# A score and value stage of one fused kernel: one factor ahead, a gram matrix in 32-column blocks, a softmax in halves

## The reference, cut to what matters

```python
xn = _inorm(xa, norm1_w, norm1_b)
k = _fno_layer(xn, Kcw, Ksw, Hs, Ws)
q = _fno_layer(xn, Qcw, Qsw, Hs, Ws)
v = _fno_layer(xn, Vcw, Vsw, H, W)
scores = jnp.einsum('bntk,bnsk->bnts', qf, kf) / (np.float32(np.sqrt(Hs * Ws)) * temperature)
p_attn = jax.nn.softmax(scores, axis=-1)
av = jnp.einsum('bnts,bnsk->bntk', p_attn, vf)
p = _fno_layer(av, Pcw, Psw, H, W)
```

## Time and profile before

| what | us |
|---|---|
| median of 3 runs | 1069.66 |
| lowest, highest | 1069.3, 1073.97 |
| the profiled execution, its own time | 1070.72 |
| its span, first to last instruction | 1069.1 |
| score stage, first load issue to the meeting | 113.7 to 186.8 |
| value stage | 186.9 to 373.5 |

### The profile page before, as it was taken

How to read it: one execution, slowest core, us unless ns; L and a number is a source line. 1 busy time by engine, 2 the same in 40 slices (tenths; PEclk the granted TensorE clock), 3 DMA queues, 4 the chain that set the end, 5 groups by cost and what they waited for, 6 DMA issues and landing times. The chain is left out here.

```text
span 1069.1 us, 36892 instructions
## 1 busy us (share of the span) xinstructions
PE 799.1 (75%) x16113; PEld 589.4 (55%) x16113; DVE 678.4 (63%) x1459; ACT 403.4 (38%) x915; POOL 368.1 (34%) x262
## 2 busy tenths in 40 slices
PE   0499296989999846999905999366677777777797
PEld 0365142322222216888705999366666667666686
DVE  4897388778888784566568999635544444553132
ACT  0298252122323263555533666323333333331121
POOL 0022373889999801111100000324434444442000
PEclk9999598899999967999957999788888888988899
DMA  9566633465555230454122665769999999997687
GB/s 364 112 188 160 137 73 104 148 255 190 182 176 183 97 79 22 155 129 114 42 67 79 175 182 158 161 153 272 262 262 266 265 266 266 269 268 164 182 243 216
DMA packets 270336, 189.43 MB, mean 177 GB/s; under 512 B 29396, under 2 KB 259509, under 8 KB 269045
## 3 DMA queue, kind: packets, MB, share of 16 engines
q1 hardware_dynamic: 190003, 131.56, 45.9%
q10 hardware_dynamic: 75138, 44.14, 17.1%
q0 software_dynamic: 5120, 12.75, 4.2%
HBM read 154.50 MB, written 33.07 MB: 175 GB/s over the span
## 5 line engine op out<-in xcount | busy, mean ns | idle before, releaser
L2035 PE MATMUL po<-pa,room 128*32 128x16 f32 x8320 | 148.0, 220 | 85.7 <-DMA room<-_L_conv_weight_imag_dram 59.0
L2035 PEld LDWEIGHTS po<-pa,room 128*32 128x32 f32 x8320 | 145.2, 163 | 94.0 <-issue 78.9
L981 POOL TENSOR_TENSOR q<-lead 128x1536 f32<-128x1536 f32 (+1 forms) x51 | 170.2, 3365 | 28.0 <-POOLq L650 13.8
L1080 DVE TENSOR_TENSOR q<-pw,lead 128x1536 f32<-128x1536 f32 (+1 forms) x85 | 140.6, 1704 | 15.7 <-PE acc L1026 10.2
L2176 DVE TENSOR_TENSOR osl<-po,neg 128x128 f32<-128x128 f32 x64 | 18.4, 287 | 151.2 <-ACT neg L2109 151.2
L1026 PE MATMUL acc<-q,pt 128*32 128x384 f32 (+1 forms) x1088 | 102.4, 486 | 14.3 <-DVE q L1080 14.3
L1988 POOL DMA_DIRECT2D os_<-osl x64 | 45.3, 713 | 184.0 <-DVE osl L2187 176.1
L1978 POOL COPY cols<-y 128x512 f32<-128x512 f32 x32 | 38.3, 1197 | 145.2 <-POOLq L1744 139.8
L2109 ACT ACTIVATE neg<-po 128x272 f32<-128x272 f32 x32 | 12.7, 397 | 199.7 <-issue 184.7
L2022 PE MATMUL px<-wbat,cols 128*32 128x130 f32 x2176 | 76.3, 293 | 3.0 <-DVE wbat L2147 3.0
L1026 PEld LDWEIGHTS acc<-q,pt 128*32 128x32 f32 x1088 | 27.5, 109 | 87.1 <-issue 57.2
(11 more groups left out here) (335 smaller groups left out, 1582.5 us busy)
## 6 DMA issues: line engine op xcount, KB each, us to landing
room<-_L_conv_weight_real_dram ACTq DMA_DIRECT2D x32, 520.0 KB, 9.8
room<-_L_conv_weight_imag_dram ACTq DMA_DIRECT2D x32, 520.0 KB, 12.6
room<-_L_conv_weight_real_dram SPq DMA_DIRECT2D x32, 520.0 KB, 7.1
room<-_L_conv_weight_imag_dram SPq DMA_DIRECT2D x32, 520.0 KB, 10.4
lead<-xns SPq DMA_DIRECT2D x64, 192.0 KB, 3.1
lead<-wv SPq DMA_DIRECT2D x16, 576.0 KB, 5.9
yall<-in_x_dram SPq DMA_DIRECT2D x4, 2048.0 KB, 14.5
xd<-in_x_dram SPq DMA_DIRECT2D x16, 512.0 KB, 4.2
```

What stands on the lines that cost most here:

```text
L981: nc.gpsimd.tensor_tensor(q2[:, t % 2, :, :, 0:m], bc(weights(blk, n), 2, NB), spectra(blk), ALU.mult).then_inc(s_qp, 1)
L1080: V.tensor_tensor(q1[:, t % 2, :, :, 0:m], bc(pw[t % 4][:, 0:3 * m].rearrange("p (r m) -> p r m", r=3), 2, NB), spectra(blk), ALU.mult).th ...
L2035: e = nc.tensor.matmul(po[u][32 * g:32 * g + 32, 512 * q + 16 * m:512 * q + 16 * m + 16], wsl[u][:, :, q * KWF + KWF - 1 - kw], xsl[u][:, ...
```

## The change

- The `vsel` steps leave the head of DVE's list and stand behind its second product. DVE signals the sum factor by itself; ACT's copy of it is signalled by itself; the two negations move behind step 1 on ACT, and only chunk 4 waits for them.
- Two gram columns (`FRONT`) are transposed ahead of the first chunk and multiplied ahead of the first scores; 2 columns stand beside each of the first 7 steps and 1 beside the next 17.
- A gram step is four matmuls of 32x32 on the diagonal blocks. Their sum lies in `pgr[:, 0:32]`, and DVE reads it there, without the copies.
- The softmax works in halves of 16 heads; the exponential overwrites the scores; `prob` lies in `room`; ACT copies both halves of `pt`.
- PE makes the first four spreads behind the last scores. POOL makes products 0 and 1 of block 0 (groups 2 and 4) as soon as that block is loaded, and DVE product 0 (into `q0`) behind the softmax, all before the engines meet.
- Block 0 takes its groups in the order 0, 2, 4, 1, 3, 5, 6, 7, with the skip sums behind group 4; ACT copies the skip sums and the offset.

```diff
-            BESIDE = [2 if j < KW - NZ + 2 else 1 if j < NZ - 2 else 0 for j in range(NZ)]
+            FRONT = 2
+            BESIDE = [2 if j < KW - FRONT - NZ + 2 else 1 if j < NZ - 2 else 0 for j in range(NZ)]
...
+                pool.wait_ge(s_blk[0], 16 * (NB + 1))
+                for t in range(2):
+                    nc.gpsimd.tensor_tensor(q2[:, t], bc(weights(0, t), 2, NB), spectra(0), ALU.mult).then_inc(s_qp, 1)
...
-                act.activation(xr[:, 1, 0:RW], xr[:, 0, 0:RW], ACT.Copy)
-                act.activation(xr[:, 1, RW:2 * RW], xr[:, 0, 2 * RW:3 * RW], ACT.Copy, scale=-1.0)
-                act.activation(xr[:, 1, 2 * RW:3 * RW], xr[:, 0, RW:2 * RW], ACT.Copy, scale=-1.0).then_inc(s_fac2, 1)
+                act.activation(xr[:, 1, 0:RW], xr[:, 0, 0:RW], ACT.Copy).then_inc(s_fac2, 1)
...
-                    nc.tensor.matmul(pgr[:, 0:NI], xg[:, kw % 2, 0, :], xg[:, kw % 2, 1, :],
-                                     start=(kw == 0), stop=(kw == KW - 1)).then_inc(s_gr, 1)
+                    for b in range(NB):
+                        i = slice(32 * b, 32 * b + 32)
+                        m = nc.tensor.matmul(pgr[i, 0:NT], xg[:, kw % 2, 0, i], xg[:, kw % 2, 1, i], start=(kw == 0), stop=(kw == KW - 1))
+                    m.then_inc(s_gr, 1)
...
+                for half in range(2):
+                    n = slice(NHD // 2 * half, NHD // 2 * (half + 1))
+                    dve.wait_ge(s_zu, NZ - 1 + half)
+                    ch.link(V.tensor_tensor(sco[:, n], sco[:, n], psc[:, 512 * half:512 * half + 512].rearrange("p (n s) -> p n s", s=NT), ALU.add))
+                    ch.link(V.reduce_max(mx[:, n], sco[:, n], axis=AX.X))
+                    V.tensor_tensor(sco[:, n], sco[:, n], bc(mx[:, n], 2, NT), ALU.subtract).then_inc(s_mx, 1)
...
+                for half in range(2):
+                    n, q = (slice(w // 2 * half, w // 2 * (half + 1)) for w in (NHD, NCK))
+                    dve.wait_ge(s_mx, half + 1)
+                    dve.wait_ge(s_ex, half + 1)
+                    ch.link(V.reduce_sum(mx[:, n], ex[:, n], axis=AX.X))
+                    ch.link(V.reciprocal(mx[:, n], mx[:, n]))
+                    V.tensor_tensor(by_head[:, q], exk[:, q], bc(mxk[:, q], 3, NT), ALU.mult).then_inc(s_p, 1)
+                dve.wait_ge(s_w3, 1)
+                dve.wait_ge(s_blk[0], 16 * (NB + 1))
+                V.tensor_tensor(q0, bc(pw[0][:, 0:3 * MB].rearrange("p (r m) -> p r m", r=3), 2, NB), spectra(0), ALU.mult).then_inc(s_q, 1)
...
-            MIX_AT = (3, 6)
+            MIX_AT, MIX_FIRST = (3, 6), (5, 6)
+            FIRST_ORDER = (0, 2, 4, 1, 3, 5, 6, 7)
```

More of the change, by code:

```diff
@@ L835, in scores @@
                     m.then_inc(s_zu, 1)
+                pe.wait_ge(s_xn, 1)
+                pe.wait_ge(s_xh, 1)
+                for kw in range(FRONT):
+                    gram_transpose(kw)
                 pe.wait_ge(s_fac, 1)
@@ L843, in _ @@
                         region(j // 2 + 1)
+                    if j == 0:
+                        for kw in range(FRONT):
+                            gram_step(kw)
                     for kw in beside(j):
@@ L1014, in _ @@
                     wait(pe, s_ac, blk - 1)
-                    for k in range(NCK):
+                    order = range(NCK) if blk else FIRST_ORDER
+                    mix_at = MIX_AT if blk else MIX_FIRST
+                    for k in order:
                         if k in POOL_K:
```

182 lines of the change are left out of this document (99 added, 83 removed).

## The result

| | before | after |
|---|---|---|
| median | 1070.61 us (1068.10 to 1074.65, 20 runs) | 1065.06 us (1062.36 to 1068.45, 20 runs) |
| ratio, 95% interval | | 0.995 (0.9939 to 0.9962) |
| span of the profiled execution | 1069.1 us | 1063.2 us |

The 20 runs of the kernel before, of which the forecast knew the first three, have a median 0.95 us above that of those three. The gain is in the stages that the change touches, but it is shared out over them otherwise than forecast, and behind them, where the code is untouched, 3.2 us were given back in the profiled execution.

A forecast was written before the change was run, and what follows sets the result against it. PE, then PE and DVE nearly level, bound the score steps, a plain chain the softmax, POOL the value stage. Score stage -3.4, softmax +2.9, value stage -2.8 sum to -3.3 us: 1066.4 us, range 1061.5 to 1070.5.

The forecast's parts named there:

- The start of the score stage: Front of the score stage: DVE scales earlier, POOL's sum ends sooner, scores 0 start at 125.2, a gain of 2.6 us.
- The score steps: Score stage: gram in blocks shortens cold steps by 0.5 and warm by 0.15; with the start 3.4 us earlier, bounds 1.9 and 5.1.
- I let the clock rise at 133, as it does now: Score steps: clock rise unchanged, so step 2 runs cold and 2.0 us of the gain are left at step 3.
- Then PE is freed a little below DVE's own 1.62: 0.2: Score steps from step 8 on: PE's pace falls just below DVE's 1.62 us, gaining only 0.2 us.
- The softmax: Softmax with POOL's products beside it: the engines meet 2.9 us later, bounds 2.5 and 4.0; without blocking 2.0 sooner.
- The lock: Softmax: a DVE instruction with both inputs in SBUF and a POOL instruction reading SBUF wait each other out.
- The value stage: Value stage: POOL's fifth product 3.7 us ahead, loads 2.8 sooner, block 3's wait grows to 4.8; gain 2.8, bounds 2.3 and 3.7.
- What comes after: Stages behind the value stage: untouched, shift rigidly, so every microsecond won or lost passes through to the end.
- the case's own low bound: Whole kernel: best ends of the three terms, -5.1 + 2.5 - 3.7 = -6.3 us, or 1063.4 us.
- 1, no blocking: Softmax: POOL and DVE do not block each other, softmax gains 2.0, total -8.2 us, 1061.5 us; chance 0.16.
- 2, the value stage keeps nothing: Value stage: block 3's landing follows the DMA queue's whole load, so total -0.5 us, 1069.2 us; chance 0.09.
- 3, the clock stays down: Score steps: clock stays at 0.50 longer, 1.4 us more per cold step, 1077.6 us with eight; chance 0.07.

The follow-up runs named there:

- e4: The changed kernel with no gram columns ahead of the first scores (FRONT 0 in place of 2); 1067.56 us, ratio 0.9956.
- a0: The changed kernel itself measured once more, unedited, as base for the follow-up runs; 1066.53 us, ratio 0.995 against the kernel before.
- e6: The changed kernel with block 0's groups in natural order 0 to 7 and the skip sums behind group 1; 1066.83 us, ratio 0.9947.
- e5: The changed kernel with the gram step as one 128x128 matmul again and the four diagonal block copies on DVE; 1070.97 us, ratio 0.9986.
- e1: The changed kernel with POOL's first two products of block 0 moved back behind the meeting of the engines; 1065.33 us, ratio 0.9929.
- e10: As e8, with the softmax's addition, maximum and subtraction also reading and writing PSUM; 1057.23 us, ratio 0.9854 against the kernel before.
- e2: The changed kernel with ACT writing the exponentials into PSUM, where DVE sums and multiplies them; 1064.29 us, ratio 0.9933.
- e8: The changed kernel with exponentials in PSUM and the two large loads parted, behind blocks 4 and 6; 1060.66 us, ratio 0.9879 against the kernel before.

## Why the prediction was right, point by point

**The start of the score stage: right.** Forecast 2.6 us earlier with POOL still the releaser; measured 2.65. POOL's sum took 4.73 us (4.53 forecast); it starts 0.21 us before DVE's sum of the low frequencies (L929, two inputs in SBUF, to 118.59) ends, and from that end it took 4.52. e4 confirms that all work of PE ahead of the first scores is hidden.

**The score steps: the mechanism right, two terms mis-sized.** Forecast 3.4 us for start and steps, with 5.1 as the high bound; measured 7.1 (56.39 to 49.26).
- "I let the clock rise at 133, as it does now": it rose near 127.4, so that scores 1 ran mostly at the high clock and step 2 wholly, and step 3 started at 131.00, 14.78 us behind the spectra against 19.11. That is 4.3 us gained where the text kept 2.0. The text gave 1.7 us as the price of a rise 2 us sooner and had it as a bound; it was 2.3. The rise came about 12.1 us behind the spectra in a0, and later still in e4 and e6, so a microsecond of this is the execution's.
- From step 3 to step 8 another 1.2 was forecast, and 1.2 came. A pair of gram columns takes 0.49 to 0.61 us warm (forecast 0.56) and 0.47 to 0.76 cold (forecast 0.72).
- "Then PE is freed a little below DVE's own 1.62: 0.2" is the other term that was mis-sized. 1.62 is the length of one product, but products in a row stand 1.545 us apart, the end of one lying over the start of the next. So the 1.64 of the earlier trace rows was PE's pace, and from step 8 to the end 1.6 us were gained. e5 shows both paces side by side. The earlier trace rows had a sign of it: DVE's 24.98 us busy of 25.90 is not what an engine at its own limit shows.
- The rule of the Trainium skill on small matmuls ("TensorE: Matmul & The Clock Gate", section "Wait — 56ns, not 53.3ns?"), which spoke against the blocks, is not contradicted: 16 passes in 0.49 us are 31 ns each, above its 25 ns. What was drawn from it, a sum poorer by 0.9 us, did not come.

**The softmax: the mechanism right.** Forecast 2.9 later with bounds 2.5 and 4.0; measured 2.2, just outside them, and 2.5. The lock was forecast at 4.9 us (2.0 sooner without, 2.9 later with it); e1 and e10 have the softmax at 11.4 us without, 2.2 sooner, and so the lock costs 4.4 to 4.7. The order of the blocked steps was forecast as in a0 (second subtraction, first multiply). In the first trace POOL came a microsecond later and caught both multiplies instead, at the same price. The mixing matrix, 1.64 us beside POOL at 189.62, is one more such step, and a forecast one would have to count; it hides.

**The value stage: the mechanism right, its end not.** The fifth product of POOL was forecast 14.9 us behind the meeting, and stands 14.8 behind it; block 2's load was forecast 2.8 sooner and came 3.4 sooner, the wait at block 3 ended 3.3 sooner and was 4.35 us long (4.8 forecast). The stage then gained 4.2 us in the executions that kept the clock (182.6 to 182.7) and 1.4 to 1.7 in the two of the changed kernel and in e2, where it fell in the wait for block 3. That is less than the 2.3 which the text had as its low bound: it saw that wait grow and gave it no second price. And the moved work is not a gain in itself: by e1, POOL's products save 4.8 here and cost 4.7 in the softmax, and by e6 the order is worth nothing.

**What comes after: not rigid.** "I let every microsecond won or lost here pass through to the end" failed in the profiled execution by +3.2 us, through the clock in the stretch behind, and it is named at the end of the text as what would make it wrong. The medians hold it less: 6.3 us in the stages, 5.5 at the end.

**The sum.** Forecast -3.4 + 2.9 - 2.8 = -3.3. Measured -7.1 + 2.2 - 1.4 = -6.3 in the stages, and -5.5 between the medians. That the time came out within 1.3 us of the forecast is in part luck: a term that was too small by 3.7 us (the score steps) met losses that were not in the sum (the clock, twice) and a median of the kernel before that lay 0.95 us higher. The stages reached the -6.3 of the case's own low bound, but not by its terms: -7.1 and -1.4 both lie outside the bounds that the text gave them.

**The rivals.** 1, no blocking, falls by e1, e2 and e10. It gave the softmax 2.0 us sooner than in the kernel before, and with the cause removed (e10) it is 2.2 sooner. 2, the value stage keeps nothing, falls by the trace, though the fall of the clock takes two thirds of the gain away. 3, the clock stays down, falls: it rose earlier.

## What to carry to other kernels

Before giving GpSimd work beside VectorE, list the VectorE instructions there that take both inputs from SBUF, and put one of them into PSUM: here the same overlap was worth nothing with two SBUF inputs and some 4 us with one (sums of e1, a0 and e2, one execution each). Take an engine's own pace from instructions that follow each other without a wait, not from the length of one, and call an engine the bound only where its busy time fills the stretch. A wait for a load can have a second price in the clock behind it, and large loads that are not urgent are best issued one at a time between the small ones that are.

## What the runs showed of the hardware

- The lock works on both sides: DVE's 512-column multiplies go from 1.07 to 3.3 us, its second subtraction from 0.69 to between 2.5 (e5) and 3.8 (e4), and POOL's two products from 6.84 to between 7.25 and 8.00. Short steps are caught too: two 32-column ones of `value_selection` (L916, L918) take 1.09 and 1.19 us beside POOL's products, and 0.19 before. Sums, maxima and reciprocals of one input were caught in none of these softmaxes.
- Whether the granted clock falls behind an idle stretch of PE is not set by its length alone: with 2.45, 2.37 and 2.15 us it was at 0.50 for 6 to 7 us (a0, e2, e1), with 2.38 and 2.18 us it stayed at 1.00 (e4, e6), at the same place of the program.
- Some 50 us behind the value stage, in unedited code, the clock falls in both kernels behind an idle stretch of 3.84 (before) and 4.25 us (changed), and stays at 0.50 for 3.4 us in the one and 9.9 in the other, which costs 3.2 us.
- Two loads of 2112 KB issued in a row make the block behind them wait 3.4 to 4.6 us wherever they stand (block 3 or 5); with one at a time (e8, e10) POOL waited for none.
